# Two low parts of one slot's weights made by GpSimd, and ScalarE's tanh ahead of a turned copy in another slot

## The reference

```python
x = x + softmax(mask(rope(q) @ rope(k).T * scale)) @ v @ w_out.T     # q from layernorm(x), k and v from the context
probs = softmax(x @ w_router); top 4 of 128, normalised                # choice of each token
gate, up = x @ w_gate, x @ w_up            # 8 shared basis units of 256, and 2 more for the shared expert
basis = silu(gate) * up
mix = (amplitudes ** 2).sum(-1), normalised over the 8 units           # weights of the units of each expert
out = sum over the chosen experts of coeff * ((mix . basis) @ w_down) + shared expert
x = x + out
```

## Time and profile before

| what | value |
|---|---|
| median of three runs | 806.81 us (805.35 to 808.48) |
| the profiled execution's own time | 806.48 us |
| its span, first to last instruction | 804.8 us |
| TensorE matmul, busy | 777.0 us (97%) |
| VectorE, busy | 647.3 us (80%) |
| ScalarE, busy | 575.6 us (72%) |
| GpSimd, busy | 535.4 us (67%) |
| mean granted TensorE clock | 0.995 of full |

### The profile page before, as it was taken

The page is one execution under the profiler, slowest core; times in us unless marked ns, Lnnn a source line. Parts: engine busy times, 40 slices in busy tenths (PEclk is TensorE's granted clock), DMA queues, the critical chain, the costliest instruction groups (busy, mean ns, idle before and its releaser), DMA issues. The chain is left out here.

```text
span 804.8 us, 15604 instructions
## 1 busy us (share of the span) xinstructions
PE 777.0 (97%) x4336; PEld 621.9 (77%) x4336; DVE 647.3 (80%) x1639; ACT 575.6 (72%) x1409; POOL 535.4 (67%) x685
## 2 busy tenths in 40 slices
PE   7788899999999999999999999999999999999998
PEld 6665677877777877777778778787778887788886
DVE  6768987899888877889788787888788787688774
ACT  3878787788876867788778767787777775654552
POOL 4586599783797769775687859776565615662572
PEclk9999999999999999999999999999999999999999
DMA  8323243654555456454445445444545345454550
GB/s 293 123 68 98 75 142 127 199 155 148 172 178 177 126 173 233 154 164 166 160 163 177 152 153 191 169 155 152 182 162 177 117 133 185 157 180 134 206 202 34
DMA packets 57053, 127.04 MB, mean 158 GB/s; under 512 B 10920, under 2 KB 28040, under 8 KB 56968
## 3 DMA queue, kind: packets, MB, share of 16 engines
q1 hardware_dynamic: 56968, 126.04, 46.9%
HBM read 107.55 MB, written 4.46 MB: 139 GB/s over the span
## 5 line engine op out<-in xcount | busy, mean ns | idle before, releaser
L1673 PE MATMUL u<-w_h,t_h 128*128 128x512 f32 x640 | 257.7, 403 | 0.7 <-issue 0.4
L1673 PE MATMUL u<-w_l,t_h 128*128 128x512 f32 x640 | 250.5, 391 | 0.0
L1673 PE MATMUL u<-w_h,t_l 128*128 128x512 f32 x640 | 250.5, 391 | 0.0
L1301 DVE TENSOR_TENSOR w_l<-w_raw,w_h 128x512 fp32r<-128x512 f32 x288 | 241.4, 865 | 0.3 <-ACT w_h L961 0.3
L961 ACT ACTIVATE w_h<-w_raw 128x512 fp32r<-128x512 f32 x380 | 216.7, 621 | 8.2 <-DMA w_raw<-in_w_units 7.0
L915 POOL TENSOR_TENSOR w_l<-w_raw,w_h 128x512 fp32r<-128x512 f32 x96 | 139.0, 1448 | 97.0 <-ACT w_h L961 96.9
L996 ACT ACTIVATE scores<-scores,mx 128x384 f32<-128x384 f32 (+1 forms) x224 | 128.8, 575 | 70.3 <-DVE mx L1244 69.0
L923 POOL TENSOR_TENSOR macc<-macc,gb 128x256 f32<-128x256 f32 x112 | 107.1, 960 | 58.5 <-DVE gb L1408 57.9
L1673 PEld LDWEIGHTS u<-w_h,t_l 128*128 128x128 f32 x640 | 120.2, 188 | 26.9
L1244 DVE CUSTOM_DVE_ANT_0 scores<-s,mask_qk 128x384 f32<-128x384 f32 (+1 forms) x224 | 112.3, 503 | 34.7 <-PE s L1549 33.4
L1673 PEld LDWEIGHTS u<-w_h,t_h 128*128 128x128 f32 x640 | 120.6, 188 | 25.3 <-issue 2.6
(11 more groups left out here) (155 smaller groups left out, 1216.6 us busy)
## 6 DMA issues: line engine op xcount, KB each, us to landing
w_raw<-in_w_units SPq DMA_DIRECT2D x160, 512.0 KB, 4.1
w_raw<-in_w_out_t SPq DMA_DIRECT2D x16, 512.0 KB, 4.4
w_raw<-in_shared_w_down SPq DMA_DIRECT2D x16, 512.0 KB, 4.6
q_st<-turned_h SPq DMA_DIRECT2D x224, 32.0 KB, 2.8
out<-x SPq DMA_DIRECT2D x16, 256.0 KB, 2.2
q_st<-turned_l SPq DMA_DIRECT2D x112, 32.0 KB, 2.8
x<-in_x SPq DMA_DIRECT2D x3, 1024.0 KB, 9.1
k_st<-turned_h SPq DMA_DIRECT2D x48, 32.0 KB, 2.8
```

The costliest lines, as they stand in the source:

```text
L1301: e.tensor_tensor(w_l[:, i % WR, k, :], w_raw[:, i % WR, k, :], f32(w_h[:, i % WR, k, :]), ALU.subtract).then_inc(s_wl, 1)
L1673: last = e.matmul(u_bank[n % 2][:], t[:, k, cols], ww[:, i % WR, k, :], start=(k == 0 and m == 0), stop=(k == KC - 1 and m == 2))
```

## The change

Two tables of one entry each are added. `POOL_LOW_TOO` gives the low parts k = 0 and k = 1 of the chunk of slot 44 to GpSimd in place of VectorE, in the same slot (42) of that engine's program. `TURN_BEHIND_TANH` makes ScalarE issue the turned copy of slot 51 behind `inverse_out` and the tanh. `weights_split` counts the low parts anew, so that each wait still names the right one.

```diff
--- before.py
+++ after.py
@@ -46,6 +46,8 @@
 UNREAD = {-5: dict(scores=6), 1: dict(scores=6), 5: dict(probabilities=10), 12: dict(probabilities=4), 15: dict(scores=2, turn=3),
           19: dict(inverse=3, scores=4), 21: dict(scores=8), 26: dict(probabilities=8), 28: dict(maxima=5),
           36: dict(scores=5), 38: dict(route=4, probabilities=3), 39: dict(route=4), 40: dict(maxima=5)}
+POOL_LOW_TOO = (44, 0), (44, 1)
+TURN_BEHIND_TANH = (51,)
 ROUTER_SPLIT, DOWN_SPLIT = (33, 35), 62
 HIGH_DVE, EARLIER_LOW, LATER_RESIDUAL = {1: 36}, {1: (3, 2)}, START[0] + 2
 LOADS, XLOAD, SELECT = (-7, 2, -3), 8, 1
@@ -542,9 +544,11 @@
 
         def weights_split(i, k):
 
-            if k in POOL_LOW:
-                return s_wlp, i * len(POOL_LOW) + sum(j in POOL_LOW for j in range(k + 1))
-            return s_wl, i * (KC - len(POOL_LOW)) + sum(j not in POOL_LOW for j in range(k + 1))
+            made = [c for s in slots for c in splits(s, "low") if low_on_pool(*c) == low_on_pool(i, k)]
+            return s_wlp if low_on_pool(i, k) else s_wl, made.index((i, k)) + 1
+
+        def low_on_pool(i, k):
+            return k in POOL_LOW or (chunk_slot[i], k) in POOL_LOW_TOO
 
         def high_made(i, k):
 
@@ -930,7 +934,7 @@
                 if (u := of_span(s, "spread")) is not None:
                     spread_inverse(u)
                 for i, k in splits(s, "low"):
-                    if k in POOL_LOW:
+                    if low_on_pool(i, k):
                         weights_low(i, k)
                 if (g := mixture(s, "scales")) is not None:
                     norm_scale(g)
@@ -1086,12 +1090,16 @@
                     maxima_out(u)
                 for u in attended_before(s):
                     out_high(u)
-                for n in tiles_in(s, "turn"):
-                    high(n)
+                if s not in TURN_BEHIND_TANH:
+                    for n in tiles_in(s, "turn"):
+                        high(n)
                 if (u := of_span(s, "inverse_turn")) is not None:
                     inverse_out(u)
                 if s - 1 in fillers and fillers[s - 1][0] == "unit":
                     tanh(fillers[s - 1])
+                if s in TURN_BEHIND_TANH:
+                    for n in tiles_in(s, "turn"):
+                        high(n)
                 if (g := mixture(s, "route")) is not None:
                     logits_low(g)
                 if (g := mixture(s, "normalize")) is not None:
@@ -1479,7 +1487,7 @@
                 if (u := of_span(s, "inverse")) is not None:
                     inverse(u)
                 for i, k in splits(s, "low"):
-                    if k not in POOL_LOW:
+                    if not low_on_pool(i, k):
                         weights_low(i, k)
 
 
```

## The result

| | before | after |
|---|---|---|
| median of 22 runs each | 806.67 us (804.95 to 808.48) | 808.28 us (806.81 to 811.33) |
| the profiled execution's own time | 806.48 us | 807.71 us |
| its span | 804.8 us | 806.0 us |
| mean granted TensorE clock | 0.995 | 0.994 |

The ratio of after to before is 1.0023, with a 95% interval of 1.0014 to 1.0031: some 1.6 us slower, a difference that so many runs show and that lies inside the half per cent. The forecast was 807.7 us.

What follows compares the result with a forecast made beforehand. ScalarE's clock at 100.81 us was taken to set TensorE's time up to slot 46. 806.48 + 1.06 - 0.2 = 807.3 us for the profiled execution, 806.81 + 0.86 = 807.7 against the median; range 805.2 to 809.8.

Steps and rivals of the forecast that it cites:

- The hold-up: Slot 42: GpSimd's low parts hold up VectorE's L1365 and L1367, so `mx` is out at 99.29, not 97.28.
- TensorE's new wait: TensorE's second `pass_a` at about 98.53 waits for `mx` to about 99.4, +0.9 us.
- ScalarE's lateness: ScalarE's instruction at 100.81 comes 2.0 - 0.41 - 0.53 = 1.06 us later, and its unbroken chain with it.
- its lower bound: Edit one with no holding up at all: -0.62 us, from 0.53 of idle time and 0.09 of overlap.
- The term that was mis-sized: GpSimd's low part 3 about 1.7 us later, rotary work behind it: costed at nothing, a few tenths if cover is gone.
- The tanh: Slot 51: tanh ahead of the copy lets the gate start earlier; TensorE gains 0.2 us at slot 52, between 0 and 0.4.
- Sum: Whole kernel: 806.48 + 1.06 - 0.2 = 807.3 us for the profiled execution; 806.81 + 0.86 = 807.7 for the median.
- the range given for it: Bounds for edit one, the two low parts: from -0.62 to +1.5 us, with +1.06 taken.
- No hold-up: Slot 42: the holding up does not bite, VectorE's slot 43 starts 1.28 us earlier; time 806.0 us; chance 0.15.
- only L1365 held: Slot 42: L1367 gets in ahead of low part 1, `mx` 0.92 us late; time 806.5 us; chance 0.17.
- The clock: TensorE's clock falls from 98.7 on for 3.4 us: +1.1 to +1.7, about 809.2 us; chance 0.10, 0.03 with a second fall.

Runs made afterwards that it cites:

- the kernel with two more reads: Before, with two added GpSimd additions of two SBUF tiles (128x512 each, result unused) at slot 42; one run, 811.82 us.
- the memsets: Before, with two added GpSimd memsets (128x512 each, of an unused buffer) at slot 42; one run, 808.27 us.
- the parts behind the coefficients: After, with GpSimd's two low parts made to wait for VectorE's last coefficient; 806.22 us, ratio 0.9998 to before.
- the three with the moved maxima: After with slot 45's `maxima_split` ahead of the gate: low parts on GpSimd behind the coefficients (805.64 us, again 805.13), or both left on VectorE (806.21).
- the moved maxima without parts: After with both low parts left on VectorE and slot 45's `maxima_split` ahead of the gate; 806.21 us, ratio 0.9998 to before.

## Why the prediction came out right, point by point

- **The hold-up** was right in each step. L1373 ended 0.28 us behind the first low part (96.91 and 96.63); the second low part ended at 98.05, on before's clock 98.20, forecast 98.19; L1375 at 98.07, 0.02 behind it; `mx` was out at 99.15, on before's clock 99.30, forecast 99.29. The experiments turned this from a reading of two other places into something shown: parts moved off the coefficients cost nothing, dummy reads hold VectorE up for the same time, and writes without reads leave the subtraction alone.
- **TensorE's new wait** for `mx` was 0.72 us, forecast 0.9; its step came at 99.45 on before's clock, forecast about 99.4.
- **ScalarE's lateness** was 0.86 us, forecast 1.06 (101.67 against 101.87 on before's clock). I subtracted the two idle times alone. But an instruction that follows another at once also starts up to 0.1 us ahead of the other's end, and one that has idled does not: from `row_sum` to `row_sum` are 2.33 us in after, and 3.49 - 0.41 - 0.53 = 2.55 in before. Each idle time used up gave 0.1 us more than itself. The prediction has this overlap of 0.09 us in its lower bound and left it out of its sum.
- **The term that was mis-sized** is the one on GpSimd: "GpSimd's low part 3 starts about 1.7 us later ... Its rotary work behind has to be turned by TensorE only after 109. I cost both at nothing; if the cover is gone, it is a few tenths." It measured 0.66 us. The low part 3 did start 1.48 us later (101.39 against 100.06), because its high part is made before the second of ScalarE's two idle times, which would have absorbed 0.6 of it. I looked for who waits for GpSimd's results, found that nobody does before 109, and left it. What I had not asked is whom GpSimd holds up by the mere time at which it works, though the whole forecast rested on just that 13 us earlier. Its next low part came 1.54 us later, at 108.80, and lay on top of `maxima_split`, which ScalarE's chain alone would have had there at 108.93; in before it had lain 0.81 us ahead of the same operation and held it for 0.35, as these two rows of its timelines of GpSimd and VectorE show. The first half of `maxima_split` ended 0.03 us behind that low part in both kernels. So the turn at slot 46 goes by GpSimd's time, 1.52 us later, and not by ScalarE's. That was so in before already: the prediction explains the 0.6 us wait for `mhl` by ScalarE's chain alone ("through tanh, gate and `mhl`"), and 0.35 of it was GpSimd's. With the hold-up taken away the turn came 1.02 us earlier, the 0.66 and before's own 0.35, which shows the term; it was then lost again to a wait for GpSimd at slot 56. Its size is less sure than its presence, since one execution of before's work had slot 46's mark 0.24 us earlier.

```profile
107.41 1.29 POOL L915 TENSOR_TENSOR w_l<-w_raw,w_h 128x512 fp32r<-128x512 f32 x1
```
```profile
108.22 0.51 DVE L1253 TENSOR_SCALAR mhl<-mx 128x8 fp32r<-128x8 f32 x1
```

- **The tanh** brought 0.28 us in this pair of traces (0.2 to 0.4 over the pairs), forecast 0.2: it ended at 129.97, the copy waited 0.88 us behind it, and TensorE's wait fell to 0.12 us, forecast 0.2.
- **Sum:** 0.86 + 0.66 - 0.28 = 1.24 by slot 53, and 1.38 at the end, forecast 0.86. For the profiled execution the forecast was 807.3 and 807.7 came; for the median 807.7, and 808.28 came. Against the 0.86 us by which the change was to be slower, the traces show 1.38 and the medians 1.61: the direction and the first mechanism were right, the size was not. ScalarE's term was 0.20 us too large, which hid a part of the term on GpSimd; that the forecast came so near owes something to this. The 1.52 us of the first edit also lie at the very end of the range given for it (+1.5).
- **The rivals.** No hold-up, and only L1365 held: both refuted by the rows above. The clock: from 99 to 103 us TensorE was busy 3.10 of 4 us at a granted clock of 1.00, so it did not fall. That it can fall here is shown by the kernel with two more reads, in which it went to the lower level at 101.1 for some 10.2 us, behind waits of 0.78, 0.17 and 0.87 us; such a fall would have cost more than the 1.7 us that the rival had for 3.4 us of it. The stretch of after:

```profile
99.00:103.00 4.00, 3.10 (x14) 2.33 (x14) 3.76 (x16) 3.81 (x9) 1.61 (x2) 1.00 0.66 237
```

The Trainium skill, page "SBUF — State Buffer", section "Who interferes with whom", says that a Vector instruction with two SBUF inputs contends with a GpSimd instruction that reads SBUF and not with one that only writes, and that `tensor_scalar` contends when it is in a two-port mode. The runs agree for the first: 0.43 us beside the memsets and 1.35 beside the reads. For the second they show 0.48 us beside the memsets, 1.24 beside the reads and 0.10 for one element; which mode these operations were in no run shows.

## What to carry to other kernels

When work moves to an idle engine, ask what the neighbour does in those microseconds, and ask it again at each later operation whose time moves with it, not only for those whose result somebody waits for: here the second such meeting cost almost as much as the first. The remedy was one wait that puts the moved work behind the neighbour's short critical operations, and a critical operation put ahead of a longer one; together they turned a loss of 1.6 us into a gain of 0.9 to 1.5 us by the medians (0.5 to 1.0 by the ends of the traces). An idle time of ScalarE that was used up gave about 0.1 us more than its length.

## What the runs showed of the hardware that was not expected

- A GpSimd memset of 128x512 (0.52 us each) left a VectorE subtraction of two SBUF tiles alone and held a two-element `tensor_scalar` to its end; the one-element form and the reciprocal were not held even by GpSimd's reads.
- Between the last two steps of the rotary work GpSimd was idle for 0.14 us in before and in five of the others (the tanh alone, the parts behind the coefficients, and the three with the moved maxima), and for 0.43 to 0.45 us in after and the remaining five. In these latter six the step before ended later than in any of the other six, but the wait in front does not grow with the lateness. What it is stays open. It carries 0.29 us of GpSimd's 1.54 us of lateness in after.
- From SyncE's issue of the last DMA of the earlier turned tile to the copy in slot 51 that waits for it, ten of twelve traces show 3.33 to 3.59 us and two 4.23 and 4.32 (the memsets, and the moved maxima without parts). In the first of the two long ones TensorE waited 0.96 us at slot 52 and in the second 1.08 us. One trace of a kernel is therefore no measure for a few tenths at slot 52. It is none at slot 46 either, where the same work gave 17.48 and 17.72 us; at slot 44 three traces agree to 0.02 us (11.30, 11.31, 11.32).
